# TensorE signals its rank and comparison groups in the sort by source with a drain instead of the last matmul

## The chip, the cores and the metric

One core of a Trainium2 chip. Each engine (TensorE or PE, VectorE or DVE, ScalarE or ACT, GpSimd or POOL, and SP, which issues DMAs) runs its own program and waits for the others by semaphores. The metric is the device time of one execution in microseconds, the median over the runs; lower is better.

## The reference

A graph network of four residual layers on 3125 nodes with 256 features and 100000 edges that are sorted by destination:

```
edge_index = jnp.stack([src, dst])
h = relu(layernorm(x));  x = x + gat_two_layers(h, edge_index)          # softmax over the edges of a destination
h = relu(layernorm(x));  x = x + dot_attention(h, src, dst)             # the same, with dot products of 8 heads
h = relu(layernorm(x));  x = x + edge_messages(h, edge_index, edge_attr_64)
h = relu(layernorm(x));  x = x + gat(h, edge_weight, row=src, col=dst)  # softmax over the edges of a source
```

The last layer sums over the edges of a source, so the kernel needs the edges sorted by source too. This sort is computed on the chip; it has no output of its own, but the last layer reads what it writes.

## The kernel before

The edges lie in 784 tiles of 128 (one edge for each partition). `sort_by_source` finds for every edge its place in the order by source, and writes its record (four numbers) there. The source's number is split into a low digit of 7 bits (128 values) and a high digit (25 values, the node's block). It goes in three parts, each a block that all engines enter and leave together:

1. `setup` loads and transposes the edges.
2. The counting loop (L334 on) makes one-hot rows and lets TensorE count, for each of 98 blocks of 8 tiles, how many edges of a smaller low digit each block of nodes has. Each of its matmuls (L339) reads a tile whose address comes from the loop's register.
3. The ranking loop (L395 to L576) is the part that the diff touches. One step is a block of 8 tiles, in two halves `j` = 0, 1 of `HB` = 4 tiles. There are 98 of them: two run ahead as a prologue, 96 in a `Fori` loop of 48 iterations with two steps each, and the last two are written out behind the loop. A step is called a turn below.

In a turn the engines do this:

- DVE: `lot` (L455, one-hot rows of the low digit) and `base` (L458) two turns ahead; `pick0` (L442) and `place0` (L447), which take the rank of half 0 out of PSUM and sum it up to a place; `rest` (L466), which completes the operand of the comparison two turns ahead; `pick1`, `place1`; `pos` (L473) and `now` (L476), which store the places.
- ScalarE: `high` (L532), `keep1` and `keep0` (L541), which take the comparison's result out of PSUM as `before`, and `recs` (L548).
- TensorE, in this order: `rank0`, `compare1` of the next turn, `rank1`, `compare0` of the turn after that. A compare group has two matmuls with fixed addresses and 256 columns (L506) and four of 178 columns (L510); a rank group has four matmuls of 25 columns (L494) whose operand `ohh[:, tile(...)]` is addressed by a register.
- GpSimd: three indirect DMAs of 128 records each (L566, the scatters of the first `SOON` = 3 tiles), when `now` and `recs` are there and the records of two turns before have landed (L576).
- SP: the load of the low digits as rows (L410).

Who waits for whom: `compare0` two turns ahead waits for `rest` (and `pick0`), `compare1` for `rest` and `pick1` of a turn before; a rank waits for its `keep`; `pick` waits for its rank, `keep` and `lot` for their compare. All of TensorE's signals go by one semaphore, `mat`. An object `Ops` counts them: `did(name, instruction)` makes an instruction raise the engine's semaphore, and `at(name, turn)` is the count at which that is done:

```
        def did(self, name, instruction):
            assert self.names[self.k] == name, (self.names[self.k], name)
            instruction.then_inc(self.sem, 1 + self.behind)
            self.k, self.behind = (self.k + 1) % len(self.names), 0
```

The records of the other five tiles of each block are scattered later, by GpSimd in the layers' stages. After the sort come `units`, the layers' node stages (`renew`) and five loops over the edges (`attend` for three of them, `attend_dot`, `aggregate_edges`), in which GpSimd gathers the rows of nodes for 808 units of 128 edges each. Each stage ends with a barrier of all engines.

Of the kernel before, what the change touches and what calls it, by code (L numbers as in the profile page):

```python
# [16 lines left out]
P = 128  # L17
# [10 lines left out]
NB = -(-N // P)  # L28
# [43 lines left out]
def gnn_kernel(nc, x_in, src_in, dst_in, attr_in, ew_in, W1, as1, ad1, b1, W2, as2, ad2, b2, Wq, bq, Wk, bk, Wv, bv,  # L72
# [3 lines left out]
    def sb(name, shape, dt=F32, c=ctx):  # L76
        return c.enter_context(nc.sbuf_tensor(name, shape, dt))

    def ps(name, shape, c, dt=F32):
        return c.enter_context(nc.psum_tensor(name, shape, dt))  # L80
# [77 lines left out]
    def sort_by_source():  # L158
# [4 lines left out]
        with ExitStack() as c:  # L163
            ohh = sb("ohh", [P, T, NB], BF16, c)
# [5 lines left out]
            with ExitStack() as c1:  # L170
# [105 lines left out]
                with ExitStack() as c2:  # L276
# [8 lines left out]
                    start = sb("cnt_start", [P, NB], F32, c2)  # L285
# [88 lines left out]
            v, a, m = Ops(vec, V, 2), Ops(act, A, 2), Ops(mat, M, 2)  # L374
            WB = P + 2 * NB
            HB = HALF // 2
            with ExitStack() as c2:
                lrow = sb("rnk_lrow", [P, 2, HALF * P], BF16, c2)
                both = sb("rnk_both", [P, 2, HALF, WB], BF16, c2)
                base = sb("rnk_base", [P, 2, HALF, NB], F32, c2)  # L380
                before = sb("rnk_before", [P, 2, HALF, P], BF16, c2)
# [8 lines left out]
                got = ps("rnk_got", [P, 2, 2, HB, 2 * P], c2)  # L390
                turn = lambda i, k: Turn(i, k, 2)
                LAST = BLOCKS // 2 - 1
                tile = lambda t, k, count: bass.ds(t.n * HALF + k, count)
                subs = lambda j: slice(j * HB, (j + 1) * HB)

                def run(eng, step):

                    step(turn(0, -2), True, False)
                    step(turn(0, -1), True, False)
                    with eng.Fori(0, LAST) as i:  # L400
                        for h in range(2):
                            step(turn(i, h), True, True)
                    step(turn(LAST, 0), False, True)
                    step(turn(LAST, 1), False, True)

                with nc.Block() as block:
# [77 lines left out]
                    @block.tensor  # L484
                    def _(eng):
                        eng.wait_ge(made, 2)

                        def step(t, begins, ends):
                            def rank(j):
                                if not ends:  # L490
                                    return m.skip(f"rank{j}")
                                eng.wait_ge(act, a.at("keep0", t.plus(-2)) if j == 0 else a.at("keep1", t.plus(-1)))
                                for k in range(HB):
                                    mm = eng.matmul(got[:, t.slot, j, k, P + NB:WB], before[:, t.slot, j * HB + k, :],  # L494
                                                    ohh[:, tile(t, j * HB + k, 1), :].rearrange("p o n -> p (o n)"),
                                                    start=False, stop=(k % 2 == 1), skip_group_check=True)
                                m.did(f"rank{j}", mm)

                            def compare(j, of, there, free):
                                if not there:  # L500
                                    return m.skip(f"compare{j}")
                                eng.wait_ge(vec, v.at("rest", of.plus(-2)))
                                if free:
                                    eng.wait_ge(vec, v.at(f"pick{j}", of.plus(-2)))
                                for k in range(0, HB, 2):
                                    eng.matmul(got[:, of.slot, j, k:k + 2, 0:P], ident_b[:, :],  # L506
                                               not_later[:, :].rearrange("p (o e) -> p o e", o=1).to_broadcast([P, 2, P]),
                                               start=True, stop=False, skip_group_check=True)
                                for k in range(HB):
                                    mm = eng.matmul(got[:, of.slot, j, k, 0:WB], both[:, of.slot, j * HB + k, 0:P],  # L510
                                                    both[:, of.slot, j * HB + k, :], start=False, stop=False,
                                                    skip_group_check=True)
                                m.did(f"compare{j}", mm)

                            first = begins and not ends
                            rank(0)
                            compare(1, t.plus(1), not (first and t.k == -2) and (begins or t.k == 0), not first)
                            rank(1)
                            compare(0, t.plus(2), begins, not first)

                        run(eng, step)
# [2137 lines left out]
```

## Time and profile before

| | |
|---|---|
| median of 3 runs | 7405.83 us (7404.95 to 7408.0) |
| span of the traced execution | 8931.6 us |
| busy in it: PE, DVE, ACT, POOL | 5412.5, 4963.7, 3871.5, 5847.5 us |
| mean granted TensorE clock in it | 0.745 |
| ranking loop in it, first to behind the last scatter | 213.2 to 737.0 us |

The traced execution has no time of its own beside its span; its span is 1525.8 us above the median of the runs that were timed. The profile is read with that in mind: durations of single instructions come from it, and whether its waits are also those of a timed run is a question by itself. The names are those of the program: `rnk_got` is the PSUM tile `got` of the ranking loop, `recs_s` the records in the order by source. PEld is TensorE's weight load, a name with q at its end (PEldq) is the instruction queue of that engine. "issue" as a releaser means that the engine waited for nothing that the profile shows; "remote" that the wait ended by a signal that the profile assigns to no instruction.

### The profile page before, as it was taken

The numbers are of one execution on the slowest core, as the hardware profiler recorded it, in microseconds if no ns is written. First come the engines' busy times: TensorE is split into PE (matmuls) and PEld (weight loads), VectorE is DVE, ScalarE is ACT, GpSimd is POOL, SyncE is SP. The second block draws the span as 40 slices with busy tenths as digits, with TensorE's granted clock in tenths as the row PEclk, the third lists the DMA queues.
The fourth block names the chain that finished last, engine by engine and source line by source line (L and its number), as shares of the span: only waits on it lengthen the run. The fifth ranks groups of instructions, "written<-read, shape, count | busy, mean of one in ns | idle before, by whom it ended". The sixth has DMA issues, their size and how long they took to land. (4 is left out here: it accounts for less than half of the span.)

```text
span 8931.6 us, 130458 instructions
## 1 busy us (share of the span) xinstructions
PE 5412.5 (61%) x23088; PEld 4000.6 (45%) x23089; DVE 4963.7 (56%) x11653; ACT 3871.5 (43%) x9075; POOL 5847.5 (65%) x8186
## 2 busy tenths in 40 slices
PE   6442365666535656664676666658888754666665
PEld 5431244444424444443455555435555533444443
DVE  6444355555545555554677777744444445555556
ACT  2220255455424554552244444335555533454444
POOL 0555677777747777775467666657777765777774
PEclk9555677777767777776788988868888866777777
DMA  4112233333313333331466666423333323333332
GB/s 143 49 49 52 75 95 95 95 96 95 86 44 97 96 95 95 96 97 33 127 176 178 177 176 175 129 64 99 100 101 100 101 53 101 99 99 99 98 98 74
DMA packets 580940, 894.72 MB, mean 100 GB/s; under 512 B 307359, under 2 KB 357708, under 8 KB 580448
## 3 DMA queue, kind: packets, MB, share of 16 engines
q0 software_dynamic: 245984, 649.30, 26.7%
q1 hardware_dynamic: 334448, 218.84, 8.9%
q10 hardware_dynamic: 416, 25.60, 0.9%
q8 instruction: 27, 0.44, 0.0%
q14 instruction: 65, 0.53, 0.0%
HBM read 859.36 MB, written 59.47 MB: 103 GB/s over the span
## 5 line engine op out<-in xcount | busy, mean ns | idle before, releaser
L2002 POOL DMA_INDIRECT ad_ring<-tab_qv,ad_idx x808 | 770.7, 954 | 506.4 <-issue 217.6
L1515 POOL DMA_INDIRECT at_ring_0a<-tab_s,at_idx_0a x808 | 774.3, 958 | 430.9 <-PE at_po_0a L1680 219.2
L2396 POOL DMA_INDIRECT ae_ring<-tab_a,ae_idx x808 | 777.9, 963 | 423.0 <-PE ae_po L2553 233.7
L1515 POOL DMA_INDIRECT at_ring_0b<-tab_s,at_idx_0b x808 | 772.8, 956 | 426.7 <-PE at_po_0b L1680 213.2
L1515 POOL DMA_INDIRECT at_ring<-tab_s,at_idx x808 | 780.1, 965 | 377.6 <-PE at_po L1680 183.0
L1680 PE MATMUL at_po_0a<-at_rows_0a,at_hot_0a 128*128 128x264 f32 x1616 | 625.6, 560 | 520.8 <-ACT at_hr_0a L1780 199.8
L1680 PE MATMUL at_po_0b<-at_rows_0b,at_hot_0b 128*128 128x264 f32 x1616 | 624.3, 559 | 512.2 <-ACT at_hr_0b L1780 201.7
L1680 PE MATMUL at_po<-at_rows,at_hot 128*128 128x260 f32 x1616 | 614.5, 553 | 444.5 <-DVE acc L1566 179.0
L1680 PEld LDWEIGHTS at_po_0a<-at_rows_0a,at_hot_0a 128*128 128x128 f32 x1616 | 439.3, 282 | 670.8 <-DVE acc L1566 262.0
L1680 PEld LDWEIGHTS at_po_0b<-at_rows_0b,at_hot_0b 128*128 128x128 f32 x1616 | 438.5, 282 | 662.4 <-DVE acc L1566 264.4
L1680 PEld LDWEIGHTS at_po<-at_rows,at_hot 128*128 128x128 f32 x1616 | 435.9, 280 | 586.2 <-DVE acc L1566 225.4
L2182 PE MATMUL ad_pk<-node_a,ad_hr 128*128 x1616 | 485.0, 452 | 337.6 <-issue 193.1
L2546 PE MATMUL ae_pM<-ae_we,ae_featT 64*128 64x256 f32 x1616 | 508.0, 465 | 171.3 <-issue 114.5
L1566 DVE TENSOR_TENSOR acc<-acc,at_po_0a 128x264 f32 x808 | 314.0, 422 | 483.9 <-PE at_po_0a L1680 215.1
L1566 DVE TENSOR_TENSOR acc<-acc,at_po_0b 128x264 f32 x808 | 312.9, 422 | 481.5 <-PE at_po_0b L1680 212.2
L566 POOL DMA_INDIRECT recs_s<-rnk_recs_now,rnk_pos_now x294 | 288.8, 982 | 409.9 <-DVE rnk_both L466 176.2
L2182 PEld LDWEIGHTS ad_pk<-node_a,ad_hr 128*128 128x128 f32 x1616 | 350.6, 226 | 452.2 <-issue 396.8
L1566 DVE TENSOR_TENSOR acc<-acc,at_po 128x260 f32 x808 | 307.1, 418 | 437.7 <-DMA recs_s<-rnk_recs_now,rnk_pos_now 178.8
L2553 PE MATMUL ae_po<-ae_msg,ae_hot 128*128 128x256 f32 x1616 | 464.8, 439 | 98.1 <-issue 60.9
L2506 DVE TENSOR_TENSOR ae_pre<-ae_ring,ae_pM 128x1024 f32<-128x1024 f32 x202 | 246.6, 1221 | 493.4 <-PE ae_pM L2546 187.7
L2546 PEld LDWEIGHTS ae_pM<-ae_we,ae_featT 64*128 64x128 f32 x1616 | 351.2, 229 | 314.6 <-issue 178.7
L2353 DVE TENSOR_TENSOR acc<-acc,ae_po 128x256 f32 x808 | 291.5, 416 | 297.9 <-PE ae_po L2553 218.8
(508 smaller groups left out, 14085.4 us busy)
## 6 DMA issues: line engine op xcount, KB each, us to landing
at_rr_0a<-relrow_d SPq DMA_DIRECT2D x102, 256.0 KB
at_rr_0b<-relrow_d SPq DMA_DIRECT2D x102, 256.0 KB
ad_rr<-relrow_d SPq DMA_DIRECT2D x102, 256.0 KB
at_rr<-relrow_s SPq DMA_DIRECT2D x102, 256.0 KB
ae_feat<-attr_pad SPq DMA_DIRECT2D x808, 32.0 KB
rnk_lrow<-lorow_f SPq DMA_DIRECT2D x98, 256.0 KB
attr_pad<-in_edge_attr_dram ACTq DMA_DIRECT2D x1, 25000.0 KB, 79.1
at_ring_0a<-tab_s,at_idx_0a POOLq DMA_INDIRECT x808
```

The source lines that it names most:

```text
L566: eng.indirect_dma_start(out=order["s"]["recs"], out_offset=bass.IndirectOffsetOnAxis(ap=pos_now[:, t.slot, k:k + 1], axis=0), in_=recs_no ...
L1515: eng.indirect_dma_start(out=ring[:, t.slot * STEP + u, :], out_offset=None, in_=table, in_offset=bass.IndirectOffsetOnAxis(ap=idx[:, t.sl ...
L1566: v.did(f"add{u}", eng.tensor_tensor(to, to, po[:, u % 4:u % 4 + 1, 0:W], ALU.add))
L1680: m.did(f"mm{u}", eng.matmul(po[:, u % 4, 0:W], hot[:, q % 2, j, :], rows[:, q % 2, j, :, :].rearrange("p h f -> p (h f)"), start=True, st ...
L2002: eng.indirect_dma_start(out=ring[:, t.slot * STEP + u, :], out_offset=None, in_=table, in_offset=bass.IndirectOffsetOnAxis(ap=idx[:, t.sl ...
L2182: mm = eng.matmul(pk[:, p % 2, (u % 2) * D:(u % 2 + 1) * D], hot_r[:, u // HALF, (u % HALF) * P:(u % HALF + 1) * P], k_tab[:, bass.ds(gs[u ...
L2353: own(eng.tensor_tensor(to, to, out_ps(q, j), ALU.add), False)
L2396: eng.indirect_dma_start(out=ring[:, k, :], out_offset=None, in_=table, in_offset=bass.IndirectOffsetOnAxis(ap=idx[:, k:k + 1], axis=0))\
L2506: own(eng.tensor_tensor(pre[:, q % 2, :, :].rearrange("p (a u) f -> p a (u f)", a=2), ring[:, q * QUAD:(q + 1) * QUAD, :].rearrange("p (a ...
L2546: mm = eng.matmul(pM[:, j // 2, (j % 2) * D:(j % 2 + 1) * D], featT[:, q % 2, j, :], We[:, :], start=True, stop=True)
L2553: mm = eng.matmul(po[:, (q % 2) * 2 + j // 2, (j % 2) * D:(j % 2 + 1) * D], hot[:, q % 2, j, :], msg[:, q % 2, j, :], start=True, stop=True)
```

## The change

Both helpers of TensorE's program keep their matmuls. The semaphore `mat` is no longer raised by the group's last matmul but by a drain, an instruction that computes nothing, behind it. The helper `m.did` and all counts are the same.

```
                                 for k in range(HB):
-                                    mm = eng.matmul(got[:, t.slot, j, k, P + NB:WB], before[:, t.slot, j * HB + k, :],
-                                                    ohh[:, tile(t, j * HB + k, 1), :].rearrange("p o n -> p (o n)"),
-                                                    start=False, stop=(k % 2 == 1), skip_group_check=True)
-                                m.did(f"rank{j}", mm)
+                                    eng.matmul(got[:, t.slot, j, k, P + NB:WB], before[:, t.slot, j * HB + k, :],
+                                               ohh[:, tile(t, j * HB + k, 1), :].rearrange("p o n -> p (o n)"),
+                                               start=False, stop=(k % 2 == 1), skip_group_check=True)
+                                m.did(f"rank{j}", eng.drain())
...
                                 for k in range(HB):
-                                    mm = eng.matmul(got[:, of.slot, j, k, 0:WB], both[:, of.slot, j * HB + k, 0:P],
-                                                    both[:, of.slot, j * HB + k, :], start=False, stop=False,
-                                                    skip_group_check=True)
-                                m.did(f"compare{j}", mm)
+                                    eng.matmul(got[:, of.slot, j, k, 0:WB], both[:, of.slot, j * HB + k, 0:P],
+                                               both[:, of.slot, j * HB + k, :], start=False, stop=False,
+                                               skip_group_check=True)
+                                m.did(f"compare{j}", eng.drain())
```

## Rows read from the trace of the kernel before

**Rows 1.** The page's first line.

```profile
span 8931.6 us, 130458 instructions
```

**Rows 2.** Windows: busy time (instructions) of each engine, granted clock, DMA share, GB/s.

```profile
213.20:737.00 523.80, 243.73 (x1908) 204.00 (x1907) 245.22 (x862) 152.09 (x382) 288.75 (x294) 0.51 0.17 48
```

**Rows 3.** Waits from 225 to 725 us: total us, times, longest.

```profile
DVE rnk_picked L442 <- remote: 227.2, 47, 5.3
ACT rnk_before L541 <- remote: 189.7, 77, 5.7
```

**Rows 4.** Timeline, PE and DVE: start, us, instruction, [idle before].

```profile
400.42 0.31 PE L494 MATMUL rnk_got<-ohh,rnk_before 128*128 x4
...
406.10 0.37 DVE L442 TENSOR_TENSOR rnk_picked<-rnk_got,ohh 128x200 f32<-128x200 f32 x1 [4.96 <-remote]
```

**Rows 5.** Timeline, POOL, 396 to 409 us.

```profile
397.21 0.97 POOL L566 DMA_INDIRECT recs_s<-rnk_recs_now,rnk_pos_now  x1 [3.49 <-DVE rnk_base L458]
398.48 0.97 POOL L566 DMA_INDIRECT recs_s<-rnk_recs_now,rnk_pos_now  x1 [0.30 <-issue]
...
408.04 0.97 POOL L566 DMA_INDIRECT recs_s<-rnk_recs_now,rnk_pos_now  x1 [3.47 <-DVE rnk_base L458]
```

**Rows 6.** Groups by line, POOL: count, busy us, mean ns, idle before and releasers.

```profile
L1515 POOL DMA_INDIRECT at_ring<-tab_s,at_idx x808 | 780.1, 965 | 377.6 <-PE at_po L1680 183.0 <-issue 114.5 <-DMA at_idx<-oth_s 31.9
L2396 POOL DMA_INDIRECT ae_ring<-tab_a,ae_idx x808 | 777.9, 963 | 423.0 <-PE ae_po L2553 233.7 <-issue 118.0 <-PEq L2532 53.0
L1515 POOL DMA_INDIRECT at_ring_0a<-tab_s,at_idx_0a x808 | 774.3, 958 | 430.9 <-PE at_po_0a L1680 219.2 <-issue 143.9 <-DMA recs_s<-rnk_recs_now,rnk_pos_now 41.9
L1515 POOL DMA_INDIRECT at_ring_0b<-tab_s,at_idx_0b x808 | 772.8, 956 | 426.7 <-PE at_po_0b L1680 213.2 <-issue 145.8 <-DMA recs_s<-rnk_recs_now,rnk_pos_now 36.6
L2002 POOL DMA_INDIRECT ad_ring<-tab_qv,ad_idx x808 | 770.7, 954 | 506.4 <-issue 217.6 <-DMA recs_s<-rnk_recs_now,rnk_pos_now 119.9 <-PE ad_pk L2182 93.1
L566 POOL DMA_INDIRECT recs_s<-rnk_recs_now,rnk_pos_now x294 | 288.8, 982 | 409.9 <-DVE rnk_both L466 176.2 <-DVE rnk_base L458 120.0 <-issue 65.5
```

**Rows 7.** Timeline, PE and PEld, turns before the first scatter and one behind it.

```profile
207.33 0.61 PE L506 MATMUL rnk_got<-rnk_not_later,rnk_ident 128*128 128x256 bf16 x2 [0.71 <-DVEq L1351]
207.73 0.80 PE L510 MATMUL rnk_got<-rnk_both 128*128 128x178 bf16 x4
208.18 0.35 PEld L494 LDWEIGHTS rnk_got<-ohh,rnk_before 128*128 128x128 bf16 x4
208.32 0.31 PE L494 MATMUL rnk_got<-ohh,rnk_before 128*128 x4
...
210.36 0.61 PE L506 MATMUL rnk_got<-rnk_not_later,rnk_ident 128*128 128x256 bf16 x2 [0.59 <-DVE rnk_both L466]
...
214.46 0.39 PE L506 MATMUL rnk_got<-rnk_not_later,rnk_ident 128*128 128x256 bf16 x2
214.69 0.48 PE L510 MATMUL rnk_got<-rnk_both 128*128 128x178 bf16 x4
```

**Rows 8.** Single lines, TensorE and its queue: ns min/median/max, first and last start.

```profile
L406 PEldq DRAIN  x1: 335/335/335, 725.5 to 725.5; - x1
L494 PE MATMUL rnk_got<-ohh,rnk_before x784: 173/183/228, 208.3 to 725.6; 128*128 x192, 128*128 128x25 bf16 x4
L494 PEldq FUSED_REGOPS  x768: 55/55/60, 207.6 to 718.2; - x192
L400 PEldq COMPARE_BRANCH  x48: 76/208/209, 213.2 to 719.8; - x48
```

**Rows 9.** Timeline, PE, the last group of the stage.

```profile
725.53 0.29 PE L494 MATMUL rnk_got<-ohh,rnk_before 128*128 128x25 bf16 x4 [0.30 <-ACT rnk_before L541]
```

**Rows 10.** Timeline, PEld, two groups of the counting loop.

```profile
150.40 1.12 PEld L339 LDWEIGHTS cnt_sums<-ohh,cnt_lo 128*128 128x128 bf16 x8 [0.55 <-issue]
151.70 1.11 PEld L339 LDWEIGHTS cnt_sums<-ohh,cnt_lo 128*128 128x128 bf16 x8 [0.18 <-issue]
```

## Prediction

> **What bounds the kernel now.** I read the page first. The traced execution spans 8931.6 us [rows 1], the median of the timed runs is 7405.83 us: the traced one is 1525.8 us longer. For an edit of a few hundred ns this difference decides everything, so the first question is which waits of the trace exist in a timed run.
>
> The edit touches one stage, from the first scatter at 213.2 us to 737.0 us, 523.8 us long, at a granted clock of 0.51, the lower level of 1.2 GHz [rows 2]. No engine is busy in it for more than 289 us. The chain of waits says what the others wait for: DVE's pick for 227.2 us and ScalarE's keep for 189.7 us, put down as "remote" [rows 3]. The timeline shows it: a rank group (L494) runs on PE from 400.42 to 400.73, and the pick that needs it starts at 406.10 [rows 4]. The matmuls are over and their signal comes 5.4 us late, about once in every loop iteration of two turns (47 times for the pick in 48 iterations). All engines then stand; GpSimd shows it as a hole of 3.47 us after six scatters [rows 5].
>
> GpSimd's own pace is 1.27 us a scatter (0.97 and 0.30 issue), 7.6 us for the six of two turns; with the hole the period is 10.83 us (397.21 to 408.04) [rows 5]. 294 scatters [rows 6] at 1.27 are 373.4 us of the 523.8: the hole costs 150 us.
>
> Are these holes in the timed runs? In the five gather loops GpSimd is idle before its gathers, other than for issue, for 430.9 - 143.9 = 287 us, 426.7 - 145.8 = 281, 377.6 - 114.5 = 263, 506.4 - 217.6 = 289 and 423.0 - 118.0 = 305 us [rows 6], 1425 us in all; the waits are put down to PE for the most part. With the 150 us here it makes 1575 us, some of it spent ahead of the loops. To get from 8931.6 down to 7405.8, 1525.8 us must go. GpSimd without those waits is about the only place that has so much. I take it that the late signals belong to tracing, and that in a timed run this stage goes at GpSimd's pace: 3.81 us a turn.
>
> What has to stay under 3.81 us is the other chain: PE and DVE. Before the scatters begin, the compare that waits for DVE starts at 207.33 and again at 210.36 [rows 7]: 3.03 us a turn, with matmuls as long as at the lower clock. So now 0.8 us a turn is slack. It holds because PE's groups run into each other: the rank's weights load at 208.18 while the compare's last matmul still runs to 208.53 [rows 7].
>
> **The change part by part.** It adds 392 drains, four a turn (98 turns: two ranks, two compares); the counts of signals are the same, no wait, DMA or buffer changes. SP's and GpSimd's queues are not passed. 
>
> What stands behind each drain. A rank group needs its addresses computed: each of its four matmuls has a register operation before it (L494 x768, 55 ns), each iteration a branch of 208 ns (L400) [rows 8]. Today all that runs while the array works off the group before. How long it takes bare is shown by the counting loop (L339), built alike, where the sequencer is the bound: eight weight loads in 1.12 us, so 0.14 us from one to the next, 0.18 us idle for "issue" between two groups, and 0.55 us where the loop turns back [rows 10].
>
> Sum for a turn at 1.2 GHz:
> - compare, twice: lead 0.25 (0.18 and the drain's own fetch), 1.21 from its first weight load to the end of its last matmul (207.33 to 208.53 [rows 7]), drain 0.05: 1.51 us;
> - rank, twice: lead 0.25, three steps of 0.14, the last matmul 0.19 [rows 8], drain 0.05: 0.91 us, where it now adds some 0.3;
> - the loop's turn: 0.55 - 0.18 = 0.37 for two turns, 0.19.
>
> 2 x 1.51 + 2 x 0.91 + 0.19 = 5.03 us. The DVE side does not add to it: from rank0's end (208.63) pick, place and rest are done for the compare at 210.36, 1.7 us, while PE spends 1.51 + 0.91 us on compare1 and rank1. ScalarE's keeps feed ranks a turn later. So the chain becomes PE alone, end to end, and passes GpSimd's 3.81 us.
>
> 98 turns at 5.03 from 207.6 end at 701 us; the last turns have fewer compares (-4.5 us), then come pick, place, now and three scatters (1.8 + 3.8 us): 702 us. Before, at GpSimd's pace: 213.2 + 373.4 + 1 = 588 us. Difference +114 us. Everything behind the stage is held by its barrier and moves as it is. Against the median, since the traced span carries the holes: 7405.8 + 114 = 7520 us, +1.5%.
>
> Bounds of that cost. Upper: two ALU operations more a group in the lead, 0.1 us four times, 40 us: 7560. Lower: the array at 2.4 GHz, where a compare takes 0.71 us (214.46 to 215.17 [rows 7]): 4.03 us a turn, 0.22 over GpSimd's, +21 us. I hold to the lower clock, since the stage had it with the same matmuls in 5.4 us a turn, which is near 5.03. The bare issue is 1.6 us of the turn (2 x 0.46 in ranks, 2 x 0.25 ahead of compares, 0.19); if it takes half of that untraced, the turn is 4.2 us, +38 us.
>
> The Trainium skill (PSUM — Partial Sum Buffer, section "Engine vs sequencer instructions") wants the increment on the matmul itself and keeps a drain for a standalone barrier, since it waits for the engine to go fully idle; the trace agrees, by the 335 ns record [rows 8]. Its page TensorE: Matmul & The Clock Gate, "Single matmul latency", gives some 183 ns beyond the streaming for a lone matmul at the lower clock; taken as the whole price of a drain, an estimate from it is 4 x 0.18 = 0.73 us, a turn of 3.5 to 3.8, which is the rival below.
>
> **Rivals.**
> - *Hidden (within 0.2%).* The sequencer decodes ahead of a drain, or the bare issue is far quicker untraced, so only the tail of each group is exposed: 2 x 1.21 + 2 x 0.40 (a weight load of 0.1 ahead of its 0.31) + 4 x 0.05 = 3.4 us, under GpSimd's 3.81. Then 7406 us, up to +10. 
> - *Late signals are real (faster).* If a timed run has the holes too, the stage lasts 5.4 us a turn before. The drain takes the signal off the matmul, and if the sequencer's signal is not late, the turn is 4.1 to 5.0 us: -30 to -125 us, 7280 to 7375 us. It decides where the hole exceeds 1.2 us a turn. For it: it is what the trace shows, 47 times. Against: the 1525.8 us that have to go somewhere.
> - *Small loss.* The upper clock or quick issue: +15 to +60 us, 7420 to 7465 us. It has the forecast's sign.
>
> **How the numbers follow.** Full loss (5.0 us a turn) 0.48; small loss 0.25, of which 0.02 lies under 0.2%; hidden 0.15, all but 0.01 of it within; late signals real 0.12, with a drain that cures them 0.10. 0.2% is 14.8 us, about what a measurement of this kernel tells from no change. Slower 0.48 + 0.23 + 0.01 = 0.72; same 0.02 + 0.14 + 0.02 = 0.18; faster 0.10. The predicted time is the full loss, 7520 us. The range from 7403 (hidden) to 7560 (upper bound) leaves out the faster case and what exceeds the upper bound; the likeliest case alone has 7490 to 7560.
>
> **What the profile after will show.** Right if: PE's rank group no longer loads weights under the compare before it; L494's four matmuls stretch from 0.31 to about 0.6 us; each group on PE has 0.2 us or more idle for "issue" before it; GpSimd waits a bit in every turn, not six scatters and one hole. In the trace the stage may even get shorter (about 5.1 us a turn against 5.4) if the sequencer's signals are not late there, while the timed runs get longer: that would show the lateness to be of the trace. Wrong if: the timed runs fall by tens of us (the signals are late there too), or the stage keeps GpSimd's pace with the drains in (their issue is hidden). The weakest step is the lead of 0.25 us, read from another loop and added four times a turn; the next is that 3.81 us is the timed pace.

## The result, and the profile after

The changed kernel takes 7527.43 us (7524.32 to 7530.8, 4 runs) against 7405.39 us before (4 runs): ratio 1.0166, 95% interval 1.0151 to 1.018. That is 122 us more; forecast were 114 us and 7520 us. One execution of all that are timed below, the fourth of `after_pause`, took 12405.89 us where the other three of the same kernel took 7524.11 to 7531.61; it is left out, and nothing recorded tells its cause.

The traced execution spans 7527.0 us, as long as a timed run, unlike the first trace of before [rows 1]. The ranking loop of before is therefore compared with a second trace of the same kernel (below), not with [rows 2 to 5].

GpSimd's scatters after the change, from the timeline (start, us, instruction, [idle before]):

```profile
396.54 0.97 POOL L566 DMA_INDIRECT recs_s<-rnk_recs_now,rnk_pos_now  x1 [1.32 <-ACT rnk_both L532]
397.81 0.97 POOL L566 DMA_INDIRECT recs_s<-rnk_recs_now,rnk_pos_now  x1 [0.30 <-issue]
399.08 0.97 POOL L566 DMA_INDIRECT recs_s<-rnk_recs_now,rnk_pos_now  x1 [0.31 <-issue]
402.04 0.97 POOL L566 DMA_INDIRECT recs_s<-rnk_recs_now,rnk_pos_now  x1 [1.99 <-DVE rnk_picked L442]
...
406.87 0.97 POOL L566 DMA_INDIRECT recs_s<-rnk_recs_now,rnk_pos_now  x1 [1.32 <-ACT rnk_both L532]
```

Three scatters keep their distance of 1.27 us, and then GpSimd waits, in every turn: 396.54 to 406.87 are two turns, 5.17 us each.

TensorE's matmuls in the same two turns:

```profile
396.71 0.61 PE L506 MATMUL rnk_got<-rnk_not_later,rnk_ident 128*128 128x256 bf16 x2 [0.33 <-issue]
397.11 0.80 PE L510 MATMUL rnk_got<-rnk_both 128*128 128x178 bf16 x4
398.25 0.65 PE L494 MATMUL rnk_got<-ohh,rnk_before 128*128 x4 [0.33 <-issue]
399.21 0.61 PE L506 MATMUL rnk_got<-rnk_not_later,rnk_ident 128*128 128x256 bf16 x2 [0.32 <-issue]
399.61 0.80 PE L510 MATMUL rnk_got<-rnk_both 128*128 128x178 bf16 x4
400.74 0.64 PE L494 MATMUL rnk_got<-ohh,rnk_before 128*128 x4 [0.33 <-issue]
401.59 0.61 PE L506 MATMUL rnk_got<-rnk_not_later,rnk_ident 128*128 128x256 bf16 x2 [0.21 <-issue]
401.99 0.80 PE L510 MATMUL rnk_got<-rnk_both 128*128 128x178 bf16 x4
403.12 0.60 PE L494 MATMUL rnk_got<-ohh,rnk_before 128*128 x4 [0.33 <-issue]
404.04 0.60 PE L506 MATMUL rnk_got<-rnk_not_later,rnk_ident 128*128 128x256 bf16 x2 [0.32 <-issue]
404.44 0.80 PE L510 MATMUL rnk_got<-rnk_both 128*128 128x178 bf16 x4
406.12 0.59 PE L494 MATMUL rnk_got<-ohh,rnk_before 128*128 x4 [0.88 <-ACT rnk_recs_now L548]
```

Read these against [rows 7]. There a rank's matmuls follow a comparison without a gap and take 0.31 us. Here each group ends, 0.21 to 0.33 us pass for "issue", and the rank takes 0.59 to 0.65 us. Between 404.44 and 406.12 lies the place where the loop turns back: 0.88 us. The releaser named at 406.12 (L548, over at 405.99) is not what TensorE waits for: this rank needs only a `keep` of an earlier turn.

The drains themselves (L497 those behind the ranks, L513 those behind the comparisons; ns min/median/max, first and last start):

```profile
L497 PEldq DRAIN  x196: 133/200/273, 210.2 to 707.8; - x196
```
```profile
L513 PEldq DRAIN  x196: 1118/1198/1215, 205.0 to 705.8; - x196
```

A comparison's drain begins with its matmuls (at 396.7 us for those that start at 396.71) and stands for all of the 1.2 us that they take. The rank's starts at 398.7, 0.2 us before its group's end at 398.90: its matmuls are issued one by one, and the drain begins when the last one, 0.2 us long, starts.

What waits for them, from the view of waits between 216 and 718 us (total us, times, longest):

```profile
ACT rnk_before L541 <- PEq L513: 328.5, 191, 1.9
POOL recs_s L566 <- DVE rnk_picked L442: 270.5, 49, 177.2
DVE rnk_picked L442 <- PEq L497: 199.0, 190, 1.5
PEld rnk_got L494 <- issue: 154.8, 192, 1.4
PEld rnk_got L506 <- issue: 74.2, 189, 0.4
```

ScalarE and DVE wait for TensorE's queue in nearly every half turn (191 and 190 times), GpSimd for DVE (270.5 us with 177.2 ahead of its first scatter). Outside this loop little moved: in the gather loops GpSimd's busy and idle times agree with the second trace of before to 5 us.

### The profile page after: what moved, and what is told of

It is laid out like the page before. It is cut to its first block and busy times, and to the rows that moved or that the text cites. A ratio compares the mean times of both kernels' runs of the same rounds, so it can differ in the third digit from the quotient of the medians.

```text
span 7527.0 us, 130850 instructions
## 1 busy us (share of the span) xinstructions
PE 5140.0 (68%) x23088; PEld 3796.3 (50%) x23089; DVE 5017.7 (67%) x11653; ACT 3883.3 (52%) x9075; POOL 5853.9 (78%) x8186
## 5 line engine op out<-in xcount | busy, mean ns | idle before, releaser
L1680 PE MATMUL at_po_0a<-at_rows_0a,at_hot_0a 128*128 128x264 f32 x1616 | 569.3, 520 | 369.6 <-ACT at_hr_0a L1780 305.9
L1680 PE MATMUL at_po_0b<-at_rows_0b,at_hot_0b 128*128 128x264 f32 x1616 | 568.6, 519 | 365.7 <-ACT at_hr_0b L1780 302.1
L1680 PE MATMUL at_po<-at_rows,at_hot 128*128 128x260 f32 x1616 | 568.0, 519 | 319.1 <-DVE acc L1566 284.1
L1680 PEld LDWEIGHTS at_po_0a<-at_rows_0a,at_hot_0a 128*128 128x128 f32 x1616 | 407.0, 261 | 493.9 <-DVE acc L1566 339.7
L1680 PEld LDWEIGHTS at_po_0b<-at_rows_0b,at_hot_0b 128*128 128x128 f32 x1616 | 406.9, 261 | 489.4 <-DVE acc L1566 335.8
L566 POOL DMA_INDIRECT recs_s<-rnk_recs_now,rnk_pos_now x294 | 284.4, 967 | 394.5 <-DVE rnk_picked L442 270.5
L2182 PE MATMUL ad_pk<-node_a,ad_hr 128*128 x1616 | 405.8, 395 | 226.3 <-DVE ad_prod L2079 199.4
L2546 PE MATMUL ae_pM<-ae_we,ae_featT 64*128 64x256 f32 x1616 | 454.0, 426 | 98.2 <-DVE ae_pre L2506 98.2
L2182 PEld LDWEIGHTS ad_pk<-node_a,ad_hr 128*128 128x128 f32 x1616 | 299.2, 193 | 326.8 <-issue 289.9
L2281 ACT ACTIVATE ad_hot<-iota_row,ad_nrel 128x128 f32<-128x128 f32 x808 | 257.4, 389 | 376.7 <-PE ad_po L2220 376.7
L2220 PE MATMUL ad_po<-ad_ring,ad_hot 128*128 128x264 f32 x1616 | 429.2, 405 | 12.0 <-DVE acc L2058 4.8
```

The source lines that it names most:

```text
L566: eng.indirect_dma_start(out=order["s"]["recs"], out_offset=bass.IndirectOffsetOnAxis(ap=pos_now[:, t.slot, k:k + 1], axis=0), in_=recs_no ...
L1680: m.did(f"mm{u}", eng.matmul(po[:, u % 4, 0:W], hot[:, q % 2, j, :], rows[:, q % 2, j, :, :].rearrange("p h f -> p (h f)"), start=True, st ...
L2182: mm = eng.matmul(pk[:, p % 2, (u % 2) * D:(u % 2 + 1) * D], hot_r[:, u // HALF, (u % HALF) * P:(u % HALF + 1) * P], k_tab[:, bass.ds(gs[u ...
L2220: m.did(f"mm{u}", eng.matmul(po[:, u % 4, 0:W], hot[:, q % 2, j, :], ring[:, a.slot * STEP + u, D:D + W], start=True, stop=True))
L2281: ins = eng.activation(hot[:, q % 2, j, :], iota_row[:, :], ACT.Abs, bias=nrel[:, of.slot, k:k + 1])
L2546: mm = eng.matmul(pM[:, j // 2, (j % 2) * D:(j % 2 + 1) * D], featT[:, q % 2, j, :], We[:, :], start=True, stop=True)
```

## The experiments

All times are medians; ratios are against the kernel before on the same chip, with the 95% interval.

**The kernel before, traced again.** No edit.

> The kernel before, traced once more. Theory (the holes of its first trace are no part of a timed run): span near 7400 us, the ranking loop from 213 to about 590 us, the scatters 1.27 us apart without holes. Rival (the holes belong to every traced execution of signals by matmul): span near 8930 us.

Span 7409.7 us, one timed run of 7411.52 us. Groups by line and the timeline of GpSimd:

```profile
L1515 POOL DMA_INDIRECT at_ring_0a<-tab_s,at_idx_0a x808 | 776.8, 961 | 156.3 <-issue 109.5 <-POOL at_pause_0a L1519 26.3 <-PE at_po_0a L1680 20.4
...
L566 POOL DMA_INDIRECT recs_s<-rnk_recs_now,rnk_pos_now x294 | 291.5, 991 | 264.7 <-DVE rnk_both L466 174.5 <-issue 47.7 <-DMA recs_s<-rnk_recs_now,rnk_pos_now 11.0
```
```profile
L566 POOL DMA_INDIRECT recs_s<-rnk_recs_now,rnk_pos_now x294: 964/971/1220, 211.8 to 594.5; - x147
```

The holes are gone, here and in the gather loops (156.3 us idle where [rows 6] had 430.9). This execution was timed as well as traced, so the holes are no part of the usual timed run. They are no part of every traced one either: of the twelve traces on record only the first has them. The 294 scatters go from 211.8 to 594.5 us, 1.306 us apart, 3.92 us a turn. Behind the change, the same line reads

```profile
L566 POOL DMA_INDIRECT recs_s<-rnk_recs_now,rnk_pos_now x294: 962/967/1168, 216.0 to 716.7; - x147
```

The last scatter starts 122.2 us later (4.2 us of it are there at the first one), as much as the 122 us of the timed runs; the spans of these two traces are 117.3 us apart.

**Drains behind the ranks alone, behind the comparisons alone.**

```
# rank_only: the comparison as before, m.did(f"compare{j}", mm)
# compare_only: the rank as before, m.did(f"rank{j}", mm)
```

> Drain behind the two rank groups of a turn, the comparison groups signal by their last matmul as before. Theory (PE's sequencer stands at the drain, and what it did under the array's work comes bare behind it): the rank's own register operations run under the comparison ahead of it again, so only the comparison's lead is bare, 2 x (1.20 + 0.3 + 0.05 + 0.33) = 3.8 us a turn, GpSimd's pace: 7400 to 7430 us. Rival A (each drain costs the same, by emptying the array): half of the loss, 7466 us. Rival B (the signal by a drain comes later, and the chain over DVE's pick pays for it): most of the loss stays, over 7480 us, since the pick waits for the rank.

> Drain behind the two comparison groups of a turn, the rank groups signal by their last matmul. Theory: each rank comes bare (0.33 lead and 0.64 for its four matmuls with their register operations), 2 x (1.20 + 0.05 + 0.33 + 0.64) + 0.2 to 0.3 for the loop's turn = 4.7 us a turn against 3.81: +80 to +90 us, 7485 to 7495 us. Rival A (equal price of a drain): 7466 us. Rival B (late signal for DVE's pick): the pick is signalled by a matmul here, so near 7406 us.

Ranks alone: 7404.1 us, ratio 1.0001 (0.9992 to 1.0011). Comparisons alone: 7468.94 us, ratio 1.0087 (1.007 to 1.0104). Half of the drains cost nothing and the other half 66 us, so an equal price a drain (rival A) is out, though its number for the second kernel is right by chance. A late signal (rival B) is out too: the pick hangs on a rank's drain in the free kernel, and on a matmul in the slow one. TensorE with ranks alone drained:

```profile
401.56 0.80 PE L510 MATMUL rnk_got<-rnk_both 128*128 128x178 bf16 x4
402.15 0.47 PE L494 MATMUL rnk_got<-ohh,rnk_before 128*128 x4
402.96 0.61 PE L506 MATMUL rnk_got<-rnk_not_later,rnk_ident 128*128 128x256 bf16 x2 [0.33 <-issue]
```

and with comparisons alone:

```profile
400.37 0.59 PE L494 MATMUL rnk_got<-ohh,rnk_before 128*128 x4 [0.99 <-ACT rnk_recs_now L548]
401.00 0.61 PE L506 MATMUL rnk_got<-rnk_not_later,rnk_ident 128*128 128x256 bf16 x2
401.39 0.80 PE L510 MATMUL rnk_got<-rnk_both 128*128 128x178 bf16 x4
402.53 0.63 PE L494 MATMUL rnk_got<-ohh,rnk_before 128*128 x4 [0.33 <-issue]
```

In the first the rank still runs into the comparison ahead of it. In the second it comes bare, 0.33 us late and 0.59 to 0.63 us long. GpSimd's scatters there are two turns apart at

```profile
396.81 0.96 POOL L566 DMA_INDIRECT recs_s<-rnk_recs_now,rnk_pos_now  x1 [1.47 <-DVE rnk_picked L442]
...
406.01 0.97 POOL L566 DMA_INDIRECT recs_s<-rnk_recs_now,rnk_pos_now  x1 [1.48 <-DVE rnk_picked L442]
```

4.60 us a turn, and 98 x (4.60 - 3.92) = 67 us. I had expected 80 to 90, with 4.7 and 3.81, which is too much.

**All drains, signals left on the matmuls.**

```
                                 m.did(f"rank{j}", mm)
+                                eng.drain()
...
                                 m.did(f"compare{j}", mm)
+                                eng.drain()
```

> All 392 drains, but each signal stays on the group's last matmul. Theory: the drain's stop is what costs, not who signals, so the time is that of the change, 7515 to 7530 us. Rival B (late signal): near 7406 us.

7522.21 us, ratio 1.0163 (1.0146 to 1.018). Who raises the semaphore makes no difference that this can tell: it is 5 us less than the change, 2.6 us less when each is taken against before on its own chip. The stop does it.

**TensorE's program written out.**

```
-                        run(eng, step)
+                        step(turn(0, -2), True, False)
+                        step(turn(0, -1), True, False)
+                        for i in range(LAST):
+                            for h in range(2):
+                                step(turn(i, h), True, True)
+                        step(turn(LAST, 0), False, True)
+                        step(turn(LAST, 1), False, True)
```

> The change, with TensorE's program of this loop written out, so that its addresses are fixed: no register operations, no branch; the other engines keep their loops. Theory: the rank's matmuls come without register operations (0.64 falls to 0.35 or so), the leads get shorter by the register operations in them, the loop's turn goes: 3.9 to 4.3 us a turn instead of 5.17, 7415 to 7455 us. Rival A (array emptied, whatever the sequencer does): 7527 us, no change by writing out.

> The kernel before with TensorE's program of this loop written out. Theory (GpSimd sets the pace before, and the register operations are hidden): 7398 to 7412 us, as before. Rival (writing out is worth something by itself, which hid a loss by the drains in the written-out change): 7390 us or less.

The change written out: 7403.18 us, ratio 0.9998 (0.9988 to 1.0008). Before written out: 7408.07 us, 1.0004 (0.9995 to 1.0014). The 392 drains are all there and cost nothing; the 768 register operations of L494 and the branches are gone from TensorE's rows. I had expected 10 to 50 us to be left. The timeline of TensorE in the first:

```profile
399.24 0.58 PE L506 MATMUL rnk_got<-rnk_not_later,rnk_ident 128*128 128x256 bf16 x2 [0.23 <-issue]
399.62 0.80 PE L510 MATMUL rnk_got<-rnk_both 128*128 128x178 bf16 x4
400.50 0.28 PE L494 MATMUL rnk_got<-ohh,rnk_before 128*128 128x25 bf16 x4
401.01 0.58 PE L506 MATMUL rnk_got<-rnk_not_later,rnk_ident 128*128 128x256 bf16 x2 [0.23 <-DVE rnk_both L466]
401.39 0.80 PE L510 MATMUL rnk_got<-rnk_both 128*128 128x178 bf16 x4
402.27 0.28 PE L494 MATMUL rnk_got<-ohh,rnk_before 128*128 128x25 bf16 x4
```

Comparison to comparison is 1.77 us, so 3.54 us a turn with four drains in it, under GpSimd's 3.92. The rank begins 0.08 us behind the comparison's end (400.42), not 0.33, and takes 0.28 us, not 0.64. Ahead of a comparison 0.23 us are left, although it has fixed addresses and nothing of the loop is there. This run takes away the register operations and the branch together; what each costs alone was not tried. That before written out is not faster can't tell more, since GpSimd sets its pace.

**The same with four drains a group.**

> The change with TensorE's program written out, and four drains behind each group instead of one. Written out alone it stayed at GpSimd's pace of 3.81 us a turn. Theory: bare, its PE turn is 2 x 1.77 = 3.54 us, of which two drains' own time is small; twelve more drains of 0.05 us make it 4.14 us: +32 us, 7430 to 7445 us. Rival A (the empty array, not the sequencer's work, is most of the 5.17 us, and the written-out kernel was fast for another reason): 3 x 20 us above the change's 7527, 7580 us or more.

7458.28 us, ratio 1.0069 (1.0052 to 1.0086), 55 us and not the expected 32. Its scatters, and two groups of TensorE:

```profile
397.62 1.10 POOL L576 DMA_INDIRECT recs_s<-rnk_recs_now,rnk_pos_now  x1 [0.76 <-DVE rnk_place L447]
...
406.45 1.10 POOL L576 DMA_INDIRECT recs_s<-rnk_recs_now,rnk_pos_now  x1 [0.79 <-DVE rnk_place L447]
```
```profile
398.26 0.29 PE L494 MATMUL rnk_got<-ohh,rnk_before 128*128 128x25 bf16 x4 [0.29 <-issue]
398.99 0.58 PE L508 MATMUL rnk_got<-rnk_not_later,rnk_ident 128*128 128x256 bf16 x2 [0.44 <-issue]
```

4.41 us a turn: twelve more drains made 3.54 to 4.41, 0.073 us each, where I had 0.05. TensorE's gaps say the same: 0.29 where one drain left 0.08, and 0.44 where it left 0.23, so 0.21 us for three drains. Rival A is out. 3.54 + 12 x 0.07 is 4.38, near the 4.41 of the scatters, and 184 of the gaps ahead of ranks are put down to issue and not to a wait: the 3.54 is the length of TensorE's own chain, and not only what GpSimd leaves.

**Two drains behind each group of the change.**

> The change with two drains behind each group, the second one signals. Theory: the second finds the array empty and costs its own issue only, 0.05 to 0.1 us, 392 times: +20 to +40 us, 7547 to 7567 us. Rival A (a drain costs some 0.3 us by itself): +118 us, 7645 us.

7547.15 us, ratio 1.0194 (1.0177 to 1.0211): 19.7 us over the change (21.4 when each is taken against before on its own chip), 0.05 us for each of 392 more drains, at the lower edge of what I gave. In the traces the last scatter starts 24.5 us later than after the change (741.2 for 716.7), 0.06 us a drain. The second drain of a group lasts

```profile
L498 PEldq DRAIN  x196: 13/13/13, 210.4 to 733.0; - x196
```

13 ns on the empty array; what makes up the rest of its 0.05 to 0.07 us no row says.

**A pause on GpSimd, before and after.**

```
+                                eng.memset(pause[:, t.slot, k, :], 0.0).then_inc(paused, 1)   # behind each scatter
```

(with a tile of 384 columns for each scatter of two turns, and a wait on `paused` for its reuse)

> The kernel before with a pause on GpSimd (a memset of 384 columns to a tile that nobody reads) behind each of the 294 scatters of the ranking loop. Theory (GpSimd sets the pace before): a scatter takes 0.97 + 0.49 + 0.165 instead of 1.27 us, 4.87 us a turn instead of 3.81: +104 us, 7505 to 7510 us. Rival (PE and DVE set it): GpSimd has slack, under +50 us.

> The change with the same pause on GpSimd. Theory (PE sets the pace after, 5.17 us a turn, and 4.87 fits under it): 7525 to 7535 us, as without it. Rival (the drains delay GpSimd's scatters in a chain with them): the pause adds up, 7600 us or more.

Before: 7489.45 us, ratio 1.0116 (1.0099 to 1.0133), 86 us more. After: 7525.31 us (three runs), ratio 1.0165 (1.0145 to 1.0186), as without it. In before a scatter is followed by

```profile
396.41 0.98 POOL L570 DMA_INDIRECT recs_s<-rnk_recs_now,rnk_pos_now  x1 [0.17 <-issue]
397.38 0.44 POOL L574 MEMSET rnk_pause<- 128x384 f32 x1
397.99 0.98 POOL L570 DMA_INDIRECT recs_s<-rnk_recs_now,rnk_pos_now  x1 [0.17 <-issue]
```

1.58 us from one to the next; 98 x (3 x 1.58 - 3.92) = 80 us of the 86; over the whole loop the last scatter starts 84.0 us later (678.5 for 594.5). The memset took 0.44 us, not the 0.49 that I had reckoned with, and the base was 3.92, not 3.81. The same work costs 86 us in one kernel and nothing in the other: the bound is GpSimd before, and GpSimd has slack after. That it is TensorE then is shown by the written-out kernels, in which only TensorE's program differs.

## Why the prediction was right

**The holes.** Right that the timed runs do not have them, on which all else rests. Wrong in whose they are: I gave them to tracing, and a second trace has none. The reckoning by spans (1575 us of holes for 1525.8 us of difference) did not need that. What delayed the signals in that one execution stays open; no trace shows it again.

**GpSimd's pace.** 3.81 us in the text, 3.92 measured (some scatters take 1.1 us). The last scatter ends at 595.5 us instead of 588.

**The drain itself.** 0.05 us behind the last matmul, read from one record of 335 ns. The rows do not carry this reading: the record's start, 725.5, is printed to 0.1 us, and 725.5 + 0.335 lies 0.015 us behind 725.82, give or take 0.05. That the size was right is luck in part. Double drains measured 0.05 to 0.06 us, four drains 0.073 us.

**The bare issue, the main term.** Sum and measurement a turn:
- before a group 0.25 us of lead and 0.05 of drain; measured from one group's end to the next one's start 0.33 ahead of a rank, and 0.33, 0.32, 0.21 and 0.32 ahead of the comparisons, the drain included;
- rank 0.61 in its four matmuls (0.42 + 0.19); measured 0.59 to 0.65;
- the loop's turn 0.37 for two turns; measured 0.88 - 0.33 = 0.55.

2 x 1.20 + 2 x 0.62 for the groups, 2 x 0.33 ahead of the ranks, 0.59 ahead of the comparisons and 0.28 for the loop's turn make 5.17, which the scatters show; the sum had 5.03. The largest miss in it is the loop's turn, 0.28 us where I had 0.19.

The written-out kernel splits this: 5.17 - 3.54 = 1.63 us come with the registers and the branch. The 1.6 us of the prediction agree with it in size but not in make-up, and that is luck. Term by term the difference of the two kernels is 2 x (0.25 of gap + 0.34 in the matmuls) = 1.18 us in the ranks, where I had 0.92; 0.17 us in the comparisons and ahead of them, where I had 0.50, since 0.23 us stay ahead of each comparison without any register; and 0.28 us at the loop's turn for 0.19. What is left, 3.54 against the 3.03 that I took for the chain before, is no price of the drains alone: the 3.03 holds a wait of 0.59 us for DVE [rows 7].

The times of the kernels bear out the turns: 4.60 and 5.17 us against 3.92 give 67 and 122 us, and 66 and 122 were measured. That they meet so closely is luck in part. Over the whole loop the turns are 4.57 and 5.13 us long, and the first scatter comes 1.2 and 4.2 us later than before; by the last scatter both together make 65.1 and 122.2 us.

**Both errors went the same way, and half of the larger one cancelled.** The end of the scatters was put 7.5 us too early before (588 for 595.5) and 16 us too early after (702 for 717.7). So 114 us were forecast for 122.

**The rivals.** Hidden: its price of 3.4 us a turn was near what the written-out kernel has (3.54), so it is what the change would have done without registers in the loop. It fell since the register operations and the branch come bare behind a drain: 1.63 us a turn that it put at nothing. Late signals real: no. Small loss through quick issue: no, the turns of 5.17 us account for the timed runs.

**The clock.** Half right. I read the granted clock of 0.51 [rows 2], the lower level, as the reason for the long matmuls. They are as long after the change, where the record says 1.00 (below). The durations, which the sum used, were right.

## What to carry to other kernels

In this kernel the stop of the sequencer was priced by what the sequencer had to do behind it (1.63 us of a turn), and little by the drains' own 0.05 to 0.07 us each: look for register operations and branches in the loop, and read their bare pace from a loop that is bound by them. The price counts only above the slack to the engine that sets the pace; here 392 drains are free with fixed addresses, half of them are free as they stand, and all of them cost 1.7%. When a trace's span is far from the timed runs (here 8931.6 us against 7405), take a second trace before reading its waits.

## What the runs showed of the hardware that was not expected

The granted clock of the records and the length of matmuls do not go together in this loop. Windows of one stretch in the second trace of before and in the trace after, with the clock as the third number from the end:

```profile
216.00:580.00 364.00, 220.65 (x1848) 187.78 (x1845) 248.51 (x835) 150.68 (x372) 276.28 (x279) 0.57 0.26 67
```
```profile
216.00:580.00 364.00, 256.09 (x1411) 162.01 (x1410) 189.33 (x634) 114.13 (x281) 205.14 (x212) 1.00 0.19 52
```

In both the 178-column matmul (L510) has a median of 355 ns, and after the change it is never shorter:

```profile
L510 PE MATMUL rnk_got<-rnk_both x784: 355/355/355, 205.4 to 706.6; 128*128 128x178 bf16 x196
```

Four of them take 0.80 us, so they start (0.80 - 0.355) / 3 = 0.148 us apart, 1.2 columns a ns. In [rows 7] the four at 214.69 take 0.48 us; with 0.24 us for one, the shortest in that trace, they start 0.08 us apart, 2.2 columns a ns. So after the change the matmuls run as at 1.2 GHz, the lower level, while the record gives 1.00. In the trace of `after_pause`, whose TensorE does the same work, the record gives 0.50 for the same stretch:

```profile
216.00:580.00 364.00, 256.04 (x1409) 161.86 (x1407) 214.09 (x632) 117.88 (x281) 307.54 (x423) 0.50 0.19 52
```
```profile
L512 PE MATMUL rnk_got<-rnk_both x784: 355/355/355, 205.4 to 707.3; 128*128 128x178 bf16 x196
```

The durations are the same, and so are the times of the two traced executions, 7528.79 and 7531.61 us. At the length that a comparison has in [rows 7] at 214.46 (0.71 us for 1.20) the turn would be 0.98 us shorter and the kernel, bound by TensorE here, some 96 us faster, an estimate from these rows. So in this loop the record changed from one execution to the next without the matmuls doing so. The times bear out the durations; why the record differs is open.

The other is the execution of 8931.6 us [rows 1], 1.5 ms over all timed runs of the same kernel, with DVE waiting up to 5.3 us for TensorE's signals in the ranking loop [rows 3]. Its cause is open.
